# Weaving the last layers of two batches into one instruction order

## The chip, the cores and the metric

The kernel runs on one core of a Trainium2 chip. The metric is the device time of one execution in microseconds (us): 4720.15 us is the median of three runs (4719.32 to 4720.28). Engines: PE is TensorE (matmuls and transposes; PEld its weight loads), ACT is ScalarE, DVE is VectorE, POOL is GpSimd, SP issues the DMAs.

## The reference, cut to what matters

Four batches of 750 frames (748 tokens after the first layer, T = 748, width 128) pass through four layers of attention and feed-forward. The change touches what follows layer 1, per batch:

```python
# layer 2 attention ("additive"): every query/key pair gets a small tanh network
hid  = tanh(hq[:, :, None, :] + hk[:, None, :, :] + b1)        # 16 hidden values a pair
attn = softmax(Q @ K.T / sqrt(128) + einsum(hid, W2) + b2)     # 748 x 748
h   += attn @ V
# layer 2 experts: 8 experts (128 -> 512 -> 128, gelu, gelu), gated for the whole batch
# layer 3 attention ("last"): 8 heads of width 128, causal, softmax
h   += concat_heads(softmax(q @ k.T) @ v) @ Wo.T
# layer 3 experts ("last experts"): 8 experts (128 -> 256 -> 128, relu), gated per token
```

Before each block the running sum `h` is normalised and transposed. Everything here is fp32.

## The kernel before, in words

Tokens lie in NT = 6 tiles of 128 (the last has 108), and a [128, 748] product is made in two halves of 384 and 364 columns. Every engine has one instruction queue, run in order; semaphores join them, and the order of each queue is written out by hand.

The front layers and the layer-1 experts fill the first 3020 us; the change leaves them alone. Then comes a hardware loop `tail` of B = 4 turns, one batch a turn, with four parts strictly one after the other:

- **part 0**: normalise `hn`, products `hq2`, `hk2`, `q2`, `v2`; `additive_attention`: per query tile, ACT makes 16 tanh planes [128, 748] (each holds 8 queries x 16 hidden values, `tanh_order`, L1436), and PE sums each plane into the 32 rows of the scores it belongs to (L942, a 128x32 weight; the target rows are `32 * (g // 4)`). Planes are taken in the order g = 0, 4, 8, 12, 1, 5, ...; each is consumed by two matmuls (the two halves of the scores) before the next one. Then softmax, transposes (L953) and product with V (L961). Then pooling and gating for the experts.
- **part 1**: layer-2 experts. `stream` runs PE jobs (L839) over four PSUM banks, ACT applies gelu (L1379); the weights come by DMA into two buffers. A loop of four turns with two experts each.
- **part 2**: `third_attention`: per head, the query product (L823, `fused` weights), values (L868), six score tiles (L881, diagonal mask L890), DVE maximum (L1728), ACT exponential (L1399), transposes of the probabilities (L901), DVE and ACT copy them (L1736, L1407), product with V (L911), DVE adds to `h` (L1745). Scores are made two tiles ahead of their use, in two pairs of banks; transposes have two banks of their own.
- **part 3**: last experts, relu (L1379 again), turned back by PE (L857) and added by DVE (L2151).

`fuse` (L987 to L992, ACT L1450) multiplies the query and key weights of each head, and the value and output weights, into `fused`: four heads (EARLY) behind part 0, four (LATE) behind part 1, in every turn of the loop. POOL computes the reciprocal root of each normalisation (L711), four a batch.

Of the kernel before, what the change touches and what calls it, by code (L numbers as in the profile page):

```python
# [29 lines left out]
P = 128  # L30
NT = (T + P - 1) // P
TP = NT * P
H0 = 3 * P
# [42 lines left out]
def offsets(parts):  # L76
# [12 lines left out]
    "operand_ready0", "operand_ready1", "xn_turned", "xn_copied", "first_merged", "h_final", "h_stored", "h_ready", "front_done", "h_spilled", "front_spilled",  # L89
    "xt_loaded", "base_loaded", "merged", "merged_spilled", "h_loaded", "hn_loaded", "hn_free", "out_free", "wts_free", "wts_loaded0", "wts_loaded1",  # L90
# [15 lines left out]
    "logits_ready", "exps_ready",  # L106
]

# [86 lines left out]
def causal_keys(tile):  # L195
# [5 lines left out]
LAYER3 = Attention(NT, lambda u: causal_keys(u % NT), float(D) ** -0.5, product_mask="diagonal",  # L201
                   summed=True)
# [143 lines left out]

def fuse_steps(heads):
# [10 lines left out]
def additive_groups(u):  # L358


    groups = min(P, T - u * P + 7) // 8
    order = [4 * (i % 4) + i // 4 for i in range(P // 8)]
    return [(g, g % 4 == 3 or g == groups - 1) for g in order if g < groups]


ADDITIVE = [additive_groups(u) for u in range(NT)]
AHEAD = 5
BETWEEN = 7


def tanh_order():

    for u in range(NT):
        for i, (g, _) in enumerate(ADDITIVE[u]):
            yield "tanh", u, g
            if u and i == AHEAD - 1:
                yield "exp", u - 1, None
    yield "exp", NT - 1, None
# [7 lines left out]
def audio_tower(nc, A, per_turn):  # L386

    with ExitStack() as ctx:
# [79 lines left out]
        hn = tokens(q_room[:, TPAD:TPAD + TP])  # L468
# [37 lines left out]
        fused = shared[:, E * W3_END:E * (W3_END + 2 * P)].rearrange("p (e n) -> p e n", e=E)  # L506
        natural = shared[:, E * (W3_END + 2 * P):E * (W3_END + 2 * P) + 6 * P].rearrange("p (k n) -> p k n", k=2)
# [36 lines left out]

        def keys_in(j):
            return min(P, T - j * P)

        def tanh_ring(i):

            return (hid[:, 0, :], hid[:, 1, :], masked[:, 0, :], masked[:, 1, :], flat(x1), flat(att), flat(y),  # L550
                    merged[:, 0:TP])[i % 8]
# [10 lines left out]
        def _(sp):  # L562
# [7 lines left out]
            def load(src, at, k):  # L570

                sp.wait_ge(S["wts_free"], n.take("wts_free"))
                sp.dma_start(wts[:, k, 0:src.shape[2]], src[at, :, :]).then_inc(S[f"wts_loaded{k}"], 16)
# [38 lines left out]
            def load_hn(b):  # L612
                sp.dma_start(flat(hn), saved["h"][b, :, :]).then_inc(S["hn_loaded"], 16)
# [10 lines left out]
            def experts():  # L624
                for e in range(-1, RUN + 1):
# [4 lines left out]
                    for what, *at in expert_steps(e):  # L630
# [22 lines left out]
                        elif what == "merge" and at[1] == 0 and e < RUN:  # L653
# [7 lines left out]
                            if e == RUN - 1:  # L661

                                sp.wait_ge(S["ring_done"], n.now("ring_done"))
                                load_hn(0)
                n.take("wr_free")
# [11 lines left out]
            def tail(b, following=None):  # L677
                sp.wait_ge(S["shared_free"], n.take("shared_free"))
                sp.dma_start(third_w, A["l3"].rearrange("e p n -> p e n")).then_inc(S["third_loaded"], 16)
                for stage, src in (("l2", A["l2"]), ("l4", A["l4"])):  # L680
                    with n.loop(sp, stage, E // 2, S["loop_entered"]) as pair:
                        for k in range(2):
                            load(src, pair * 2 + k, k)
                    if stage == "l2" and following is not None:
                        sp.wait_ge(S["hn_free"], n.take("hn_free"))
                        load_hn(following)
                sp.wait_ge(S["h_final"], n.take("h_final"))
                full = (NT - 1) * P
                sp.dma_start(A["out"][b, 0:full, :].rearrange("(t p) d -> p t d", p=P), h[:, 0:NT - 1, :])\
                    .then_inc(S["h_stored"], 16)  # L690
                sp.dma_start(A["out"][b, full:T, :], h[0:T - full, NT - 1, :]).then_inc(S["h_stored"], 16)
                sp.wait_ge(S["h_stored"], n.take("h_stored", 32))
                sp.sem_inc(S["out_free"], 1)

            spill_merged(STAGES[-1])
            sp.sem_inc(S["out_free"], 1)
            with n.loop(sp, "tail", B - 1, S["loop_entered"]) as b:
                tail(b, b + 1)
            tail(B - 1)
# [3 lines left out]
        def _(pool):  # L703
# [81 lines left out]
            with n.loop(pool, "tail", B, S["loop_entered"]):  # L785
                power(4)
# [3 lines left out]
        def _(pe):  # L790
            n = Tally("tensor", per_turn)

            def turn(src, waited=False):

                if not waited:
                    pe.wait_ge(S["operand_ready"], n.take("operand_ready"))
# [33 lines left out]
            def stream(jobs, start, first=0):  # L830

                base = n.now("feat_done") - first
                for i, (reads, terms, (lo, hi)) in enumerate(jobs, first):

                    pe.wait_ge(S["feat_done"], base + (max(reads, i - 3) if reads else i - 3))
                    for c, (w, rhs) in enumerate(terms):
                        mm = pe.matmul(ps[:, (start + i) % 4, 0:hi - lo], w, rhs[:, lo:hi],  # L839
                                       start=(c == 0), stop=(c == len(terms) - 1))  # L840
# [1430 lines left out]
```

## Time and profile before

| | us |
|---|---|
| median of three runs | 4720.15 |
| the profiled execution | 4720.54 |
| its span on the core | 4718.2 |
| PE busy in it | 4292.0 (91%) |
| ACT busy | 2950.9 (63%) |
| DVE busy | 2785.4 (59%) |

The profile has a page with shares, a strip of 40 slices, and views of the trace: groups by line, a timeline, waits, and busy times of a stretch. Matmul ends are modelled and neighbouring records overlap, so PE's rate is read from start to start. An fp32 matmul stands as two records, an fp32 transpose as one.

### The profile page before, as it was taken

Reading aid. Unit: us, or ns where it says so; the run is one execution under the profiler, and the core shown is the slowest. Engines: PE = TensorE matmul, PEld = TensorE weight load, DVE = VectorE, ACT = ScalarE, POOL = GpSimd, SP = SyncE. Lnnn points to the kernel's source line nnn. Section 1 sums busy time; section 2 is a strip of 40 time slices with the busy share of each in tenths; the row PEclk is TensorE's granted clock in tenths of the full one; section 3 lists DMA queues with packets and bytes.
Section 4 is the critical chain, followed back from the end, with each engine's and each line's share of the span. In section 5 each row is a group of like instructions: output and inputs, shape, how many; then the busy total and the mean of one; then the engine's idle time right before and its main releaser. Section 6 shows DMA issues by size and latency. Waiting matters only on the chain.

```text
span 4718.2 us, 71767 instructions
## 1 busy us (share of the span) xinstructions
PE 4292.0 (91%) x24891; PEld 2384.9 (51%) x24891; DVE 2785.4 (59%) x6486; ACT 2950.9 (63%) x6401; POOL 692.9 (15%) x466
## 2 busy tenths in 40 slices
PE   6888689999999999999999999789888888988988
PEld 4555434444444444444444444356645654664566
DVE  5655477777777777777777777223422542252244
ACT  2222257777777778777777777574475447537644
POOL 0000212222222222222222322100000000000000
PEclk9868789999999999999999999899999989999999
DMA  2000142424334243342424322100011010001000
GB/s 105 1 27 1 34 48 41 52 38 55 54 46 59 38 55 50 50 58 39 55 45 55 54 38 34 42 14 22 10 36 35 1 45 5 31 1 45 27 5 17
DMA packets 101136, 173.34 MB, mean 37 GB/s; under 512 B 18816, under 2 KB 75568, under 8 KB 100400
## 3 DMA queue, kind: packets, MB, share of 16 engines
q1 hardware_dynamic: 100784, 168.82, 20.7%
q8 instruction: 199, 3.26, 0.3%
q14 instruction: 153, 1.25, 0.1%
HBM read 86.66 MB, written 7.82 MB: 20 GB/s over the span
## 4 chain that ended last, share of the span: by engine, by line
PE 54%; issue 35%; DVE 6%; ACT 1%; DVEq 1%; POOL 1%; DMA 1%; POOLq 0%; SPq 0%; ACTq 0%
PE ps L1032 12%; PE ps L1068 12%; PE ps L1042 10%; PE ps L1102 4%; PE ps L1111 3%; PE ps L1023 2%; PE ps L868 2%; PE ps L1131 2%; DVE peaks L1851 1%; PE ps L823 1%; PE ps L881 1%; PE ps L1092 1%; PE ps L839 1%; PE ps L1136 1%; PE ps L911 1%
## 5 line engine op out<-in xcount | busy, mean ns | idle before, releaser
L1851 DVE TENSOR_REDUCE peaks<-ps 128x1 f32<-128x748 f32 (+1 forms) x1536 | 1408.2, 933 | 482.7 <-PE ps L1042 460.4
L1469 ACT ACTIVATE masked<-ps 128x384 f32<-128x384 f32 (+3 forms) x1536 | 683.4, 486 | 196.2 <-PE ps L1032 184.1
L1469 ACT ACTIVATE probs<-ps 128x384 f32<-128x384 f32 (+1 forms) x1536 | 662.5, 484 | 73.9 <-PE ps L1032 73.5
L711 POOL TENSOR_TENSOR rstd<-var,minus_half 128x6 f32<-128x6 f32 x104 | 138.3, 1330 | 2998.6 <-DVE var L1670 2998.6
L1032 PE MATMUL ps<-shared 98*128 98x384 bf16 (+3 forms) x1536 | 447.3, 327 | 4.4 <-ACT probs L1469 1.7
L1032 PE MATMUL ps<-q_stack,k_stack 98*128 98x384 bf16 (+3 forms) x1536 | 450.0, 328 | 1.0
L1042 PE MATMUL ps<-k_stack,q_stack 96*128 96x374 bf16 (+1 forms) x1536 | 380.6, 329 | 36.0 <-DMA k_stack<-parts 21.6
L1042 PE MATMUL ps<-shared 96*128 96x374 bf16 (+1 forms) x1536 | 372.1, 323 | 9.0 <-DVE peaks L1851 8.3
L1032 PEld LDWEIGHTS ps<-shared 98*128 98x128 bf16 (+1 forms) x1536 | 147.9, 103 | 336.6 <-ACT masked L1469 125.8
L1032 PEld LDWEIGHTS ps<-q_stack,k_stack 98*128 98x128 bf16 (+1 forms) x1536 | 149.6, 103 | 328.7 <-ACT masked L1469 121.2
L839 PE MATMUL ps<-xnT,wts 128*128 128x384 f32 (+1 forms) x768 | 270.8, 503 | 5.0 <-DVE lg L2110 3.3
L1399 ACT ACTIVATE probs<-ps,neg_top 128x128 f32<-128x128 f32 (+3 forms) x216 | 131.8, 613 | 221.1 <-DVE neg_top L1730 221.1
L839 PE MATMUL ps<-hid,wts 128*128 128x384 f32 (+1 forms) x768 | 251.7, 478 | 0.0
L1379 ACT ACTIVATE hid<-ps,wts 128x364 f32<-128x364 f32 (+1 forms) x384 | 211.1, 575 | 44.1 <-PE ps L839 31.8
L1042 PEld LDWEIGHTS ps<-k_stack,q_stack 96*128 96x128 bf16 (+1 forms) x1536 | 154.7, 105 | 158.2 <-DVE peaks L1851 43.1
L1042 PEld LDWEIGHTS ps<-shared 96*128 96x128 bf16 (+1 forms) x1536 | 155.8, 104 | 117.9 <-issue 38.5
L1102 PE MATMUL ps<-attT,wr 128*128 128x364 f32 (+1 forms) x512 | 208.2, 491 | 2.7
L839 PEld LDWEIGHTS ps<-xnT,wts 128*128 128x128 f32 x768 | 150.1, 200 | 105.1 <-issue 19.4
L839 PEld LDWEIGHTS ps<-hid,wts 128*128 128x128 f32 x768 | 145.9, 190 | 95.4 <-ACT hid L1379 0.7
L881 PE MATMUL ps<-xnT,QT 128*128 128x320 f32 (+5 forms) x512 | 174.2, 449 | 2.3 <-ACT QT L1367 2.3
L911 PE MATMUL ps<-V,probsT 128*128 128x128 f32 x936 | 151.1, 304 | 26.0 <-DVE probsT L1736 25.9
L1728 DVE TENSOR_REDUCE top<-ps 128x1 f32<-128x128 f32 (+3 forms) x216 | 129.0, 597 | 75.3 <-PE ps L890 67.5
(389 smaller groups left out, 7609.5 us busy)
## 6 DMA issues: line engine op xcount, KB each, us to landing
shared<-parts SPq DMA_DIRECT2D x192, 187.0 KB, 9.2
wr<-in_l SPq DMA_DIRECT2D x32, 580.5 KB, 3.5
q_stack<-parts SPq DMA_DIRECT2D x96, 187.0 KB, 7.9
k_stack<-parts SPq DMA_DIRECT2D x96, 187.0 KB, 10.2
wts<-in_l SPq DMA_DIRECT2D x32, 514.5 KB, 3.3
wrow<-in_l_rows SPq DMA_DIRECT2D x32, 320.0 KB, 4.1
wts<-in_l SPq DMA_DIRECT2D x32, 257.5 KB, 2.6
shared<-in_l SPq DMA_DIRECT2D x4, 2048.0 KB, 9.8
```

What stands on the lines that cost most here:

```text
L711: pool.tensor_tensor(lane.rstd, lane.var, minus_half[:, :], ALU.pow).then_inc(S["rstd_ready"], 1)
L839: mm = pe.matmul(ps[:, (start + i) % 4, 0:hi - lo], w, rhs[:, lo:hi], start=(c == 0), stop=(c == len(terms) - 1))
L881: mm = pe.matmul(ps[:, 2 * (u % 2) + a, 0:width], query(u), key(u)[:, a * width:(a + 1) * width], start=True, stop=masked_by is None, skip ...
L911: mm = pe.matmul(ps[:, 6 + u % 2, 0:dv], probsT[:, j, :], value(u, j), start=(j == 0), stop=(j == len(tiles) - 1))
L1032: pe.matmul(out[0:m, 0:hi - lo], k_stack[k][0:STACK + SHIFT, head, j * P:j * P + m], q_stack[k][0:STACK + SHIFT, head, lo:hi], start=True, ...
L1042: mm = pe.matmul(out[0:m, a, 0:T // 2], q_stack[k][0:STACK, head, j * P:j * P + m], k_stack[k][0:STACK, head, a * T // 2:(a + 1) * T // 2] ...
L1068: mm = pe.matmul(ps[at:at + PLACE, 6, 0:hi - lo], V32[x % 2][0:m, j, head, :], probs_ring(SIDE * b + i)[0:m, 0:hi - lo], start=(j == 0), s ...
L1102: pe.matmul(out[:, 0:hi - lo], wr[:, WR_UP + f * P:WR_UP + (f + 1) * P], attT[:, lo:hi], start=True, stop=True).then_inc(S["ring_ready"], 1)
L1111: mm = pe.matmul(out[:, 0:hi - lo], wr[:, WR_DOWN + f * P:WR_DOWN + (f + 1) * P], hid[:, f, lo:hi], start=(f == 0), stop=(f == FT - 1))
L1379: act.activation(dst[:, lo:hi], ps[:, (start + i) % 4, 0:hi - lo], final if f is None else func, bias=bias[-1] if f is None else bias[f]). ...
L1469: act.activation(probs_ring(u)[0:m, 0:hi - lo], src[0:m, 0:hi - lo], ACT.Exp, scale=float(HD) ** -0.5).then_inc(S["ring_done"], 1)
L1851: v.tensor_reduce(peaks[0:m, g, j, head:head + 1], src[0:m, :, 0:T // 2], XY, ALU.max)\
```

## The change

The loop is replaced by one list, `TAIL`, from which every engine writes its queue. Each part is a list of steps with costs; `woven` merges two lists so that both advance at the same relative pace. The order is: part 0 and part 1 of batch 0 alone; then for b = 1, 2, 3 part 2 of batch b-1 with part 0 of batch b, and part 3 of b-1 with part 1 of b; at the end part 2 and part 3 of batch 3 alone. No hardware loop is left.

```diff
+def woven(*parts):
+    out = []
+    for b, part in parts:
+        steps, done = tail_steps(b, part), 0.0
+        whole = sum(cost for _, cost in steps)
+        for step, cost in steps:
+            out.append(((done + cost / 2) / whole, b, part, step))
+            done += cost
+    return [(b, part, step) for _, b, part, step in sorted(out, key=lambda entry: entry[0])]
+
+def tail_order():
+    order = woven((0, 0)) + woven((0, 1))
+    for b in range(1, B):
+        order += woven((b - 1, 2), (b, 0)) + woven((b - 1, 3), (b, 1))
+    return order + woven((B - 1, 2)) + woven((B - 1, 3))
```

Two sets of buffers and semaphores (`tails`, `TailLane`) serve even and odd batches. What else changes:

- **fuse** is a step of batch 0 alone; `fused` then stays in SBUF, and the last experts' weights (`fourth_w`) are loaded once instead of per batch.
- **additive attention**: 24 `add` steps, four tanh planes each (a "quad"), in three slots of four buffers. ACT's step: four tanh; in the second of each tile two tanh, the exponential of the tile before, two tanh. PE now takes a whole quad for the first half of the scores, then for the second. PSUM: one pair of banks for scores (5, 6), one bank (7) for transposes and results:

```diff
+                    pe.wait_ge(S["hidden_ready"], n.take("hidden_ready"))
+                    for a in range(2):
+                        for i, (g, last) in enumerate(quad):
+                            at = 32 * (g // 4)
+                            mm = pe.matmul(ps[at:at + 32, 5 + a, 0:T // 2],
+                                           add_w[:, 32 - 8 * (g % 4):64 - 8 * (g % 4)],
+                                           tanh_buffers[4 * slot + i][:, a * T // 2:(a + 1) * T // 2], start=False,
+                                           stop=last, skip_group_check=True)
+                    mm.then_inc(S["hidden_used"], 1)
```

- **last attention**: 67 steps `last(i)` over a list of entries, for each head score 5, 3, 4, 0, next query, 1, next value, 2, alternating between slot X (banks 0 and 1) and slot Y (bank 2). In step i PE does: product with V of entry i-3, first-half transposes of entry i-2, entry i itself, second-half transposes of entry i-2. Transposes share one bank (4), results one bank (3). ACT in step i: copy of the second-half transposes of i-2, then the exponential (or copy) of entry i. DVE: add of i-3, copy of i-2, maximum of i. The values of a head are copied by one ACT instruction instead of six:

```diff
+                    what, e, u = last_entry(i - 3)
+                    if what == "score":
+                        slot_done(LAST_AT["value", e, None])
+                        taken(k)
+                        if tiles > 3:
+                            pe.wait_ge(S[f"taken1_{k}"], n.take(f"taken1_{k}"))
+                    spread(0)
+                    if what is not None and slot_before(i) is not None:
+                        slot_done(slot_before(i))
+                    spread(1)
```

- **layer-2 experts** keep four banks (4 to 7); **last experts** get three (0 to 2) and one (3) for turning back. Their relu and gelu now alternate in ACT's queue.
- SP's queue: the next batch's `hn` is loaded when its lane's buffer is free (`hn_free_k`), then eight expert weights, then the store of the batch before.

## Rows read from the trace of the kernel before

**Rows 1.** The page, busy time of each engine over the span.
```profile
PE 4292.0 (91%) x24891; PEld 2384.9 (51%) x24891; DVE 2785.4 (59%) x6486; ACT 2950.9 (63%) x6401; POOL 692.9 (15%) x466
```
**Rows 2.** Timeline of POOL in the tail: start us, length, engine, line, operation.
```profile
3026.66 1.33 POOL L711 TENSOR_TENSOR rstd<-var,minus_half 128x6 f32<-128x6 f32 x1 [4.42 <-DVE var L1670]
...
3450.33 1.32 POOL L711 TENSOR_TENSOR rstd<-var,minus_half 128x6 f32<-128x6 f32 x1 [67.18 <-DVE var L1670]
...
3873.33 1.32 POOL L711 TENSOR_TENSOR rstd<-var,minus_half 128x6 f32<-128x6 f32 x1 [66.74 <-DVE var L1670]
```
**Rows 3.** Stretches, parts 0 to 3: us; PE, PEld, DVE, ACT, POOL busy; PEclk; DMA.
```profile
3444.50:3567.80 123.30, 101.02 (x578) 52.65 (x578) 32.35 (x102) 91.15 (x128) 2.64 (x2) 0.91 0.09 30
3567.80:3661.50 93.70, 90.60 (x290) 55.58 (x290) 17.89 (x61) 54.10 (x95) 1.32 (x1) 0.94 0.14 44
3661.50:3801.50 140.00, 124.17 (x807) 97.54 (x808) 76.89 (x240) 59.75 (x186) 0.00 (x0) 1.00 0.00 1
3801.50:3868.00 66.50, 56.65 (x216) 38.16 (x214) 23.91 (x102) 29.26 (x51) 1.32 (x1) 0.90 0.09 24
```
**Rows 4.** Busy time by stretch, columns as above: tanh stretch; layer-2 experts at full clock.
```profile
3464.50:3544.50 80.00, 78.67 (x472) 37.05 (x472) 12.59 (x32) 77.96 (x102) 0.00 (x0) 1.00 0.00 1
...
3571.70:3651.20 79.50, 79.44 (x251) 47.05 (x249) 9.72 (x25) 45.98 (x81) 0.00 (x0) 1.00 0.15 48
```
**Rows 5.** PE's timeline where two parts join (idle before it in brackets).
```profile
3453.45 1.54 PE L799 MATMUL ps<-const,xn 128*128 128x128 f32 x6 [10.31 <-DVEq L1656]
...
3566.42 0.60 PE L1280 MATMUL ps<-const,spread 128*128 128x8 f32 x2 [5.83 <-DVEq L1656]
...
3808.39 1.54 PE L799 MATMUL ps<-const,xn 128*128 128x128 f32 x6 [5.86 <-DVEq L1656]
```
**Rows 6.** PE's timeline, first and last record of a `fuse` (half clock).
```profile
3655.00 1.54 PE L987 MATMUL ps<-const,shared 128*128 128x128 f32 x6 [0.65 <-DVE h L1714]
...
3660.75 0.39 PE L992 MATMUL ps<-shared 128*128 128x128 f32 x2
```
**Rows 7.** ACT's timeline, tanh planes back to back.
```profile
3480.67 0.90 ACT L1436 ACTIVATE y<-hid,hqb 128x748 f32<-128x748 f32 x1
3481.48 0.90 ACT L1436 ACTIVATE merged<-hid,hqb 128x748 f32<-128x748 f32 x1
```
**Rows 8.** Busy time of line L942 alone over the tanh stretch.
```profile
3463.00:3545.00 82.00, 62.75 (x376) 25.25 (x376) 1.00 0.00 1
```
**Rows 9.** PE's timeline in the experts of layer 1: four column groups together (L1068).
```profile
2591.03 0.82 PE L1068 MATMUL ps<-probs,V 128*32 128x364 f32 x8
2591.78 0.69 PE L1032 MATMUL ps<-q_stack,k_stack 98*108 98x364 bf16 x3
```
**Rows 10.** PE's timeline over one head of the last attention.
```profile
3668.40 0.33 PE L901 MATMUL ps<-const,probs 128*128 128x128 f32 x1 [0.71 <-ACT probs L1399]
...
3675.57 0.21 PE L890 MATMUL ps<-maskb,identb 128*128 128x108 bf16 x1
...
3678.37 1.38 PE L911 MATMUL ps<-V,probsT 128*128 128x128 f32 x10 [1.08 <-DVE probsT L1736]
...
3685.93 0.33 PE L901 MATMUL ps<-const,probs 128*128 128x128 f32 x1 [0.71 <-ACT probs L1399]
```
**Rows 11.** DVE's timeline in that head.
```profile
3675.82 0.94 DVE L1728 TENSOR_REDUCE top<-ps 128x1 f32<-128x748 f32 x1 [0.46 <-PE ps L890]
```
**Rows 12.** ACT's timeline in that head.
```profile
3677.02 0.88 ACT L1399 ACTIVATE probs<-ps,neg_top 128x748 f32<-128x748 f32 x1 [1.53 <-DVE neg_top L1730]
```
**Rows 13.** ACT's timeline, table loads in front of a gelu and none before a relu.
```profile
3568.77 1.28 ACT L1379 ACT_TABLE_LOAD   x1
...
3817.66 0.24 ACT L1444 ACTIVATE ex<-lg 128x48 f32<-128x48 f32 x1 [7.22 <-DVE lg L1818]
3818.96 0.58 ACT L1379 ACTIVATE hid<-ps,wts 128x384 f32<-128x384 f32 x1 [1.06 <-PE ps L839]
```
**Rows 14.** DVE's timeline at the turn of the loop `tail`.
```profile
3448.17 1.25 DVE L1662 BATCH_NORM_STATS2 stats<-q_stack 128x6 f32<-128x128 f32 x6 [3.68 <-issue]
```

More of the change, by code:

```diff
@@ L355, with additive_quads @@
 EARLY, LATE = tuple(range(E // 2)), tuple(range(E // 2, E))
-def additive_groups(u):
+def additive_quads(u):
     groups = min(P, T - u * P + 7) // 8
[L362 to L378, printed above, removed]
+    return [[(g, g % 4 == 3 or g == groups - 1) for g in range(q, groups, 4)] for q in range(4)]
@@ new lines, with last_attention_entries @@
+ADDITIVE = [additive_quads(u) for u in range(NT)]
+TANH_SLOTS = 3
+X_SLOT, Y_SLOT = 0, 1
+def last_attention_entries():
+    out = [("query", 0, None), ("value", 0, None)]
+    for e in range(E):
+        for u in (5, 3, 4, 0):
+            out.append(("score", e, u))
+        if e + 1 < E:
+            out.append(("query", e + 1, None))
+        out.append(("score", e, 1))
+        if e + 1 < E:
+            out.append(("value", e + 1, None))
+        out.append(("score", e, 2))
+    return out
@@ L381, in cut @@
+TAIL = tail_order()
+@dataclass
+class TailLane:
+    k: int
+    h: object
+    hn: object
+    xn: object
+    xT: object
+    QT: object
+    V: object
+    probs: object
+    probsT: object
+    stats: object
+    mv: object
+    var: object
+    rstd: object
+    half_sum: object
+    pooled: object
+    spread: object
+    hqb: object
+    top: object
+    neg_top: object
+    total: object
+    rtotal: object
+    gating: object
+    gates: object
+    gcol: object
 def cut(ap, n):
@@ L675, in _ @@
             experts()
[L677 to L687, printed above, removed]
+            spill_merged(STAGES[-1])
@@ L692, in tail @@
                 sp.wait_ge(S["h_stored"], n.take("h_stored", 32))
[L693 to L699, printed above, removed]
+                sp.sem_inc(S[f"out_free_{k}"], 1)
+            sp.wait_ge(S["shared_free"], n.take("shared_free"))
+            sp.dma_start(third_w, A["l3"].rearrange("e p n -> p e n")).then_inc(S["third_loaded"], 16)
@@ L784, in _ @@
             experts()
-            with n.loop(pool, "tail", B, S["loop_entered"]):
-                power(4)
+            for b, part, (what, *at) in TAIL:
+                if what == "normalise":
+                    power(1, tails[b % 2])
         @block.tensor
@@ L1537, in experts @@
                 n.take("stacks_loaded", 2 * len(Q_PARTS) * 16)
-            def columns(k, at, count):
-                return [wts[:, k, at + i:at + i + 1] for i in range(count)]
             act.wait_ge(S["consts_loaded"], 48)
@@ L1704, in tok_measured, with attention @@
                             v.bn_stats(lane.stats[:, tile, :], dst[:, tile, :])
[L1706 to L1717 removed]
+            def attention(spec, dst):
                 def peak(u):
```

1043 lines of the change are left out of this document (698 added, 345 removed).

## The prediction

> **What bounds the kernel now.** I read the page first: PE is busy 91% of the span, ACT and DVE about 60% [rows 1]. An average over unlike stages says little, so next came the tail's period. POOL does four roots per batch; the first of each batch stands at 3026.66, 3450.33 and 3873.33, so one turn takes 423.5 us and the four turns 1694 of the 4718 us [rows 2]. Then I cut one turn into its four parts [rows 3]: 123.3 us (part 0), 93.7 (part 1), 140.0 (part 2), 66.5 (part 3). They are bound differently. In the tanh stretch ACT is busy 77.96 of 80.00 us [rows 4], one plane each 0.81 us [rows 7]; in the layer-2 experts PE is busy 79.44 of 79.50 [rows 4]; in part 2 PE is busy 124.2 of 140.0 and ACT 59.8. Between the parts PE stands idle for the normalise-and-turn chain and the gating: 10.31, 5.83 and 5.86 us [rows 5], and the granted clock of these stretches is 0.90 to 0.94 instead of 1.00 [rows 3]: after each such gap PE runs a while at 1.2 GHz. So the tail has two kinds of slack: an ACT-bound part 0, and the joints.
>
> **The change, part by part.** What the weave can reach is PE's own work, so I sum PE's time for each woven pair.
>
> Tanh sums. Before, the 376 records of L942 keep PE busy 62.75 us beside ACT [rows 8]. In the new order the four matmuls of a quad go to four different groups of 32 columns, as the four matmuls (eight records) of L1068 do: the next instruction starts 0.75 us after the first [rows 9], for 364 columns in fp32. A step is two such quads; the second needs no change back to the full array, so 1.45 us a step, and 24 steps are 35 us. The bounds are 24 x 1.3 = 31 (no cost for entering and leaving) and 62.75 (no gain from the order); I take 35 because L1068 has the same shape of weight and the same order. The Trainium skill, TensorEngine Tiling (Array Packing), Key Properties, says that changing the tiling mode drains TensorE, which speaks against sprinkling quads between full-array matmuls. The 0.75 us holds such a change already, so the trace prices it below 0.15 us.
>
> The rest of part 0: PE is busy 101.0 us there [rows 3]; less 62.75 for L942 and about 4 for `fuse` (an estimate from its 6 us at half clock [rows 6]) that leaves 34. The clock of 0.91 over 123.3 us means 22 us at half clock [rows 3], mostly idle; I take some 6 us of work in them, which takes half at full clock, so 31.
>
> Woven pair W1 (part 2 of b-1 with part 0 of b): 124 + 35 + 31 = 190 us of PE. ACT: 59.8 + 91.2 - about 5 (`fuse` and a table load) - 5 (values copied at once) = 141 us; DVE: 76.9 + 32.4 = 109 us. PE bounds it, at 74% load of ACT.
>
> In-order queues cost something on top. A score tile of 748 columns goes PE to DVE in 0.25 us (3675.57 to 3675.82 [rows 10, 11]), DVE to ACT in 1.20 (3675.82 to 3677.02 [rows 11, 12]), and ACT needs 0.88: about 2.4 us until its transposes can start, behind it on ACT now four tanh, 3.24 us. I walked one query tile of part 0 (add steps 2, 3, 0, 1 and 2 again) against one head (8 steps of `last`, 15.4 us of PE work: 17.53 from start to start less the waits of 1.08 and 0.71 [rows 10], rounded down for shorter ones). PE's work is 28 us and its waits come to 3.3: 2.3 us where the transposes of a short tile wait for an exponential queued behind the add step in which ACT also does its own exponential and PE has nothing (q = 1), and twice 0.7 where the product with V follows the second-half transposes with nothing between. That is 12%, of 190 us some 22; with part of such waits already in the 124, I take 20. W1 = 210 us. Bounds: 190 (no wait) and 190 + 24 x 2 = 238 (every add step keeps PE waiting for what is left of 3.24 us after PE's own 1.45, rounded up).
>
> Woven pair W2 (part 3 of b-1 with part 1 of b): layer-2 experts 79.5 + 2 = 81.5 us [rows 4]; part 3 has 56.65 us busy, and its clock of 0.90 means 13 us at half clock [rows 3], of which about 12 are work and count half, so 51; turning back and one normalisation 1.7. Together 134 us of PE against 54.1 + 29.3 = 83 of ACT. Waits: at its end the normalisation of batch b (5.86 us of idle PE in the open today [rows 5]) has only some 4 us of the other lane's work beside it, and then the next pair waits for the copy: 4 us; 3 more for a gating exponential among the gelus and PSUM rings of four and three banks. W2 = 141, bounds 134 and 155 (all joints of today's parts 1 and 3 stay open, some 20 us).
>
> Alone at the start: part 0 and part 1 of batch 0. ACT still bounds the tanh stretch; PE now has pauses in it, which is worth 0 to +8 us if the clock falls there. I take 217 + 2 = 219. Alone at the end: part 2 of batch 3 has one bank for transposes, so the product with V waits for ACT's copy in three tiles of a head and twice for DVE's; a walk over one head (waits of 0.8, 0.7, 0.7, 0.7 and 0.4 us where 2.1 stand now) gives 18.5 us for 17.53, +8 us, bounds 0 and +16. Part 3 keeps its 66.5 (three banks are enough: a matmul takes PE 79.44 / 128 = 0.62 us [rows 4], an activation 0.58 [rows 13], and PE is two jobs ahead). So 140 + 8 + 66.5 = 214.5.
>
> `fuse` once instead of four times removes about 6 us from first to last record at half clock [rows 6], of which most lies under the normalisation chain; in the pairs it is simply left out of the sums. The loop's turn, 3.68 us of DVE idle for nothing [rows 14], goes too and is part of the joints. The loads of `third_w` and of the last experts' weights per batch go; the layer-2 weights have the same two buffers and DVE frees them as before. SP's new waits (`hn_free_k`, then eight loads, then the store) queue nothing that is needed sooner than a whole pair later: cost nothing, and 5 us a pair if a load were late.
>
> **The sum**, against the profiled execution: 219 + 3 x (210 + 141) + 214.5 = 1486.5 for 1694, 207.5 less. The profiled execution took 4720.5 (span 4718.2, 2.3 around it), the median is 4720.15, so I predict 4720.5 - 207.5 = 4513 us.
>
> **The rivals.**
> *No waits in the weave.* The quad and the other lane cover each other's round trips: W1 = 190, W2 = 134. For it: ACT is at 74%. Against: tanh blocks of 3.24 us stand ahead of exponentials that PE needs within about two steps. 3 x 27 = 81 us below the forecast: 4432.
> *ACT's queue paces the weave.* Every add step delays the other lane: W1 = 238 and W2 = 155. That is 3 x 42 = 126 above: 4639. For it: PE gets nothing in the q = 1 step, and there the walk loses most.
> *No gain from weaving.* If each pair ran like its parts in sequence, only the loop turns and three fuses would go: 4 x 3 + 3 x 3 = about 20 us, 4700. For it speaks only that both lanes share all three queues.
> *Table reloads, slower.* In W2 relu and gelu alternate on ACT. A load takes 1.28 us [rows 13] and stands wherever the function asked for is not in the loaded set. The last experts have 16 relu and 16 identity steps a pair, each between gelus: up to 64 loads, 82 us of ACT, and with the jobs waiting in turn nearly as much of PE. It decides from 207.5 / (3 x 1.28) = 54 loads a pair; at 64 the time is 4513 + 246 = 4759. Against it: relu follows an exponential without a load [rows 13]. No row has relu right after gelu. The Trainium skill, ScalarE: Activation LUTs, Table sets, says that relu, copy and identity are in every set, and also to batch calls by set; by its 1283 ns plus about 1380 ns of drain a reload would be twice as dear, 4513 + 510 = 5023 by 64 of them. The first of its sentences speaks for the change, and the trace agrees as far as it goes.
>
> **How the numbers follow.** Forecast (4460 to 4590, the pairs each within some 20 us of their sums) 0.70; no waits 0.11; ACT paces 0.13; no gain 0.03, half of it within 0.2%; slower 0.03. The range 4440 to 4620 holds the forecast, most of the first rival and half of the second, about 0.84 less what I overlook. A measurement of this kernel can tell 0.2%, 9 us, from no change. Faster 0.95, same 0.02, slower 0.03.
>
> **What would show it.** In the changed kernel's stretches: the first pair W1 of about 210 us with PE busy nearly throughout, granted clock 1.00 and ACT about two thirds busy; the records of the tanh sums starting four together, 1.4 to 1.5 us a step; no table load between relus and gelus; no idle of PE over 3 us except at the ends of W2. Waits of PE on ACT's `probs` over 2 us behind the q = 1 steps prove the walk right. The prediction is wrong if quads don't run together (W1 up by 27 us), if PE waits in most steps, or if half clock persists within the pairs.

## The result, and the profile after

The changed kernel takes 4617.27 us (median of four runs, 4615.43 to 4618.23) where the kernel before takes 4719.73 on the same chip: a ratio of 0.9782, 95% interval 0.9766 to 0.9799. That is 102.5 us less. The forecast was 207 us less, 4513; its range (4440 to 4620) just holds the result.

The page shows the same shares as [rows 1], of a shorter span:

```profile
PE 4177.5 (91%) x24723; PEld 2308.0 (50%) x24723; DVE 2783.5 (60%) x6451; ACT 2903.9 (63%) x6181; POOL 693.1 (15%) x466
```

So it tells nothing of where the gain is. POOL's roots cut the tail again, as in [rows 2] (timeline of POOL, columns as there):

```profile
3025.11 1.33 POOL L892 TENSOR_TENSOR rstd<-var,minus_half 128x6 f32<-128x6 f32 x1 [4.27 <-DVE var L2413]
3135.58 1.32 POOL L892 TENSOR_TENSOR rstd<-var,minus_half 128x6 f32<-128x6 f32 x1 [109.14 <-DVE var L2413]
...
3625.62 1.32 POOL L892 TENSOR_TENSOR rstd<-var,minus_half 128x6 f32<-128x6 f32 x1 [7.71 <-DVE var L2413]
...
4008.09 1.32 POOL L892 TENSOR_TENSOR rstd<-var,minus_half 128x6 f32<-128x6 f32 x1 [7.71 <-DVE var L2413]
...
4381.43 1.32 POOL L892 TENSOR_TENSOR rstd<-var,minus_half 128x6 f32<-128x6 f32 x1 [133.04 <-DVE var L2413]
4550.89 1.32 POOL L892 TENSOR_TENSOR rstd<-var,minus_half 128x6 f32<-128x6 f32 x1 [168.14 <-DVE var L2413]
```

Two pairs together take 4008.09 - 3625.62 = 382.5 us; the forecast had 210 + 141 = 351, and before a batch took 423.5. Part 0 alone takes 110.5 us between the first two roots, part 2 alone 169.5 between the last two; the kernel before had 103.2 and, between the like roots, 148.1. The stretches (columns as in [rows 3]) are part 0 of batch 0 alone; pair W1 (part 2 with part 0) from its first to its last step, the second of the three; pair W2 (part 3 with part 1); part 2 of batch 3 alone:

```profile
3025.11:3135.58 110.47, 79.32 (x557) 40.76 (x558) 24.55 (x68) 87.17 (x117) 1.33 (x2) 0.83 0.08 29
...
3623.70:3861.60 237.90, 200.07 (x1358) 135.67 (x1359) 112.36 (x359) 141.62 (x264) 2.65 (x2) 0.94 0.03 9
...
3862.00:3999.90 137.90, 135.28 (x465) 83.98 (x464) 33.30 (x121) 77.65 (x134) 2.15 (x2) 0.97 0.08 24
4381.43:4550.89 169.46, 135.79 (x817) 101.20 (x817) 83.54 (x267) 55.97 (x145) 1.32 (x2) 0.95 0.01 3
```

The forecast booked the joint behind W2 with W2, so the two sums compare like this: W2 with its joint takes 138 + 6 = 144 for 141, and W1 takes 238 from its first step to its last for 210, three times. The miss is in W1; the stretch alone at the end adds 20 (235 for 214.5). TensorE's six longest waits in W1 (engine, tile and line; what it waited for; us in total, times, longest):

```profile
PE ps L1543 <- ACT parts L1953: 8.3, 11, 1.8
PE ps L1557 <- DVE parts L2555: 6.7, 9, 3.3
PE ps L1543 <- DVE parts L2555: 5.8, 4, 4.1
PE ps L1557 <- ACT parts L1964: 4.7, 3, 2.7
PE ps L1579 <- ACT y L1973: 2.7, 1, 2.7
PE ps L1428 <- ACT probs L1898: 2.4, 1, 2.4
```

L1543 is the product with V, L1557 the transposes, L1579 the scores of part 2; ACT L1953 and DVE L2555 copy the transposed halves, ACT L1964 is the exponential. No single wait carries it, and busy time hides a good part, since the ends of matmuls are modelled. So I read the distances between the starts of PE's instructions and took off each the time of its size at full clock (0.83 us for 1000 columns of an fp32 record: records of 384 columns start 0.32 us apart, 0.64 at half clock; a quad of sums counts a quarter of that, as its four column groups run together). W1 in us (own calculation from the trace):

```
work by size, full clock   168
extra at half clock          9
small gaps (under 0.15)     11
waits over 0.15             49    (61 of them; before, 20 in the 140 us of part 2)
```

Without its waits the pair is 168 + 9 + 11 = 188 us, and the floor of the forecast was 190. The waits were put at 20. By place, the first 27 us of the second pair (from the end of the experts before) hold 12.6 us of work, and its last 34 us 16.7 us of work and 14 of waits. VectorE's timeline shows the last wait (14 lines of the gating and one of part 2 left out):

```profile
3854.70 0.41 DVE L2555 COPY parts<-ps 128x256 f32<-128x256 f32 x1
3855.03 0.16 DVE L2149 SCALAR_TENSOR_TENSOR lg<-pick,lg 128x8 f32<-128x8 f32 x1
...
3858.59 0.18 DVE L2142 TENSOR_TENSOR gates<-ex,m 128x8 f32<-128x8 f32 x1
...
3859.41 0.35 DVE L2549 SCALAR_TENSOR_TENSOR k_stack<-ps,wrow,k_stack 128x128 f32<-128x128 f32 x1 [0.41 <-issue]
3859.68 0.55 DVE L2555 COPY parts<-ps 128x384 f32<-128x384 f32 x1
```

and TensorE's the price:

```profile
3855.78 0.49 PE L1557 MATMUL ps<-const,parts 128*128 128x128 f32 x3
3860.38 1.62 PE L1543 MATMUL ps<-y,parts 128*128 128x128 f32 x6 [4.11 <-DVE parts L2555]
```

Transposes started at 3855.78 are copied only at 3859.68, because batch b's gating, small operations every 0.24 us, stands ahead in the queue.

### The profile page after: what moved, and what is told of

It reads as the page before. It is cut to its first block, busy times and chain, and to the rows that moved or that the text cites. A ratio compares the mean times of both kernels' runs of the same rounds, so it can differ in the third digit from the quotient of the medians.

```text
span 4615.9 us, 66988 instructions
## 1 busy us (share of the span) xinstructions
PE 4177.5 (91%) x24723; PEld 2308.0 (50%) x24723; DVE 2783.5 (60%) x6451; ACT 2903.9 (63%) x6181; POOL 693.1 (15%) x466
## 4 chain that ended last, share of the span: by engine, by line
PE 76%; DVE 9%; ACT 6%; issue 6%; DVEq 2%; POOL 1%; DMA 1%; POOLq 0%; PEld 0%; PEldq 0%; SPq 0%; ACTq 0%
PE ps L1131 12%; PE ps L1167 12%; PE ps L1487 11%; PE ps L1141 10%; PE ps L1201 4%; PE ps L1210 3%; PE ps L1122 2%; PE ps L1543 2%; PE ps L1018 2%; PE ps L1419 2%; PE ps L1579 2%; DVE peaks L2180 2%; PE ps L1230 2%; PE ps L1003 1%; PE ps L1031 1%
## 5 line engine op out<-in xcount | busy, mean ns | idle before, releaser
L1878 ACT ACTIVATE hid<-ps,wts 128x384 f32<-128x384 f32 (+1 forms) x256 | 146.3, 573 | 63.7 <-PE ps L1487 52.4
L1210 PE MATMUL ps<-hid,wr 128*128 128x364 f32 (+1 forms) x512 | 171.1, 477 | 0.0
L1487 PE MATMUL ps<-hid,wts 128*128 128x364 f32 (+1 forms) x512 | 169.5, 478 | 0.0
L1791 ACT ACTIVATE hid<-ps,wr 128x384 f32<-128x384 f32 (+1 forms) x256 | 139.9, 572 | 44.0 <-PE ps L1201 40.7
L1167 PE MATMUL ps<-masked,shared 128*32 128x384 f32 (+3 forms) x1536 | 160.5, 490 | 0.6 <-ACT masked L1750 0.6
L1167 PE MATMUL ps<-probs,V 128*32 128x384 f32 (+1 forms) x1536 | 160.5, 490 | 0.0
L1167 PE MATMUL ps<-masked,V 128*32 128x384 f32 (+3 forms) x1536 | 160.5, 490 | 0.0
L1167 PE MATMUL ps<-probs,shared 128*32 128x384 f32 (+1 forms) x1536 | 160.5, 490 | 0.0
L1487 PEld LDWEIGHTS ps<-hid,wts 128*128 128x128 f32 x512 | 96.8, 190 | 62.1
```

The source lines that it names most:

```text
L1167: mm = pe.matmul(ps[at:at + PLACE, 6, 0:hi - lo], V32[x % 2][0:m, j, head, :], probs_ring(SIDE * b + i)[0:m, 0:hi - lo], start=(j == 0), s ...
L1210: mm = pe.matmul(out[:, 0:hi - lo], wr[:, WR_DOWN + f * P:WR_DOWN + (f + 1) * P], hid[:, f, lo:hi], start=(f == 0), stop=(f == FT - 1))
L1487: mm = pe.matmul(ps[:, bank, 0:hi - lo], w, rhs[:, lo:hi], start=(c == 0), stop=(c == len(terms) - 1))
L1791: act.activation(dst[:, lo:hi], src[:, 0:hi - lo], ACT.Gelu, bias=wr[:, bias:bias + 1])\
L1878: act.activation(dst, src, func, **more).then_inc(S[f"feat_done_{k}"], 1)
```

## The experiments

Each starts from the changed kernel or from a better version named there. "Pair" is W1 from its first to its last step, the second of three. The kernel before took 4717.7 to 4720.0 in these comparisons.

**What is the weave worth by itself?** e1_sequence:

```diff
-        order += woven((b - 1, 2), (b, 0)) + woven((b - 1, 3), (b, 1))
+        order += woven((b - 1, 2)) + woven((b - 1, 3)) + woven((b, 0)) + woven((b, 1))
```

> The new parts, quads and single fuse are kept, but nothing is woven: part 0, 1, 2, 3 of each batch in turn. If the missing gain went into the new steps of parts 0 and 2 (alone in the changed kernel: start 219.3 us between POOL's roots, part 2 169.5 where 148.1 stood before), a batch costs 219.3 + 169.5 + 66 = 455 us, some 8 less where fuse is left out, and the total is 4617 + 4 x 455 - 24 - (219 + 3 x 382.5 + 235) = 4812 us: slower than before by about 90. If the new steps cost nothing and the weave itself brought only 100, it lands at about 4700 (before, less three fuses and the loop's turns).

4808.55 us, ratio 1.0189 (1.0169 to 1.0210). So the change is two changes: new parts that cost 90 us, and a weave that gives 191. The parts that were made fit for the weave cost nearly half of what it gives. Part 2 in its new order, alone, takes 166.2 us between roots (3239.22 to 3405.43) for 148.2 before.

**ScalarE's queue.** e2_half_tanh leaves out two of the four tanh planes of a step:

```diff
+                        if i % 2:
+                            continue
                         last = act.activation(tanh_buffers[4 * (s % TANH_SLOTS) + i][:, 0:T], ...
```

> ScalarE computes two of the four tanh planes of each step and leaves the others out (TensorE adds all four buffers as before, so its work is the same). A block of tanh ahead of an exponential is 1.6 us instead of 3.2. Theory 1 (TensorE's waits in the pair of part 2 and part 0 come from ScalarE's in-order queue): the pair falls from 244 us to 215-222, its waits from 48 to about 20. Theory 2 (the waits come from part 2's own order: product with V right behind the second-half transposes of the same tile): the pair falls by at most 8, to 236 or more. Part 0 alone at the start falls by some 30 us in both.

4583.28 us; the pair 231.2, 7 us less. ACT's busy time in it fell by 36:

```profile
3598.50:3829.70 231.20, 200.57 (x1358) 137.45 (x1359) 112.38 (x359) 105.21 (x218) 2.64 (x2) 0.94 0.03 9
```

By its length this speaks against theory 1; the waits alone say otherwise, see below.

**Part 2's own order.** e3_late_weigh: in a step PE did product with V of i-3, first transposes of i-2, filling of i, second transposes of i-2. Now the filling comes first, `copied` waits for both copies of i-3 (the bank is free then), and `weigh_last`, the product with V of i-3, stands between the two halves:

```diff
+        def last_probsT(lane, i):
+            return (lane.probsT, lane.xn)[LAST_UNIT[i] % 2]
...
                     if what is not None:
                         mm.then_inc(S[f"slot_ready_{k}"], 1)
                         n.take(f"slot_done_{k}")
+                    copied()
+                    spread(0)
+                    weigh_last()
                     spread(1)
```

with VectorE's copy and maximum ahead of its addition, and a second buffer for the transposed probabilities. Order and buffer are tested together.

> In each step of the last attention the product with V of tile i-3 moves from the head of the step to a place between the two transposes of tile i-2, and the filling of tile i to the head (so that a copy always has a matmul job over it); the transposed probabilities get a second buffer (the normalised rows, idle there). Theory 2 (part 2's own order): part 2 alone falls from 169.5 us to about 150, each woven pair from 244 to 225-230, total 4617 - 19 - 3 x 16 = 4550. Theory 1 (ScalarE's queue): part 2 alone falls just so, the pairs stay within 5 us each, total 4590 to 4598. If the wait is on the exponential's round trip instead, nothing changes or it gets slower by some us.

4587.29 us, ratio 0.9720 (0.9704 to 0.9736). Part 2 alone fell from 169.5 to 151.9 us between roots (4369.33 to 4521.26): that cause is shown. The pairs moved by little, the three of them by -3, -1 and -7 us: about what theory 1 says, which e2 had just spoken against. But the waits of PE in them did fall, by 8 us a pair. What took that back is the clock: the granted clock of the second pair is 0.91 for 0.94, and the extra at half clock rose from 9 to 16 us.

**The joint.** e4_joint: part 1 spread over 86% of W2, and the next batch's first normalisation inside it.

> Only the order of steps at the end of the pair of part 3 and part 1 changes: part 1 of the later batch ends after 86% of the pair, so that its normalisation lies beside the other batch's last experts, and the first normalisation of the batch after it is made there too. Theory 3 (the joint costs 5 us of idle TensorE and then 17 us at half clock): each of three joints loses 8 to 12 us, total 4617 - 25 to -35 = 4582 to 4592, and the clock at the start of the pair stays at full. Rival: the last experts alone in the rest of the pair wait for each other as the joint did, and the total stays within 5 us.

4615.95 us, nothing. The 5 us of idle PE before the joint became one wait of 2.0, one of 1.3 and one of 2.7, and PE's half clock still lay over the opening of W1, where query, value and first scores wait for each other's copies.

**The order of the planes.** e5_planes:

```diff
-                    for a in range(2):
-                        for i, (g, last) in enumerate(quad):
+                    for i, (g, last) in enumerate(quad):
+                        for a in range(2):
```

> TensorE adds the planes of a quad one after the other, two matmuls each (as before the change), and not the four planes for one half and then for the other: the same 376 instructions in another order. The forecast's term: the sums take 62 us of TensorE where they take 35 now, so each woven pair becomes 27 us longer (244 to 271, total 4617 + 3 x 27 = 4698), while part 0 alone at the start is bound by ScalarE and, with TensorE busy nearly throughout and its clock at full, gets 3 to 7 us shorter. Rival: the quads don't run together and nothing changes.

4622.19 us, 5 us more and not 81; the intervals of the two ratios overlap (0.9778 to 0.9817 and 0.9766 to 0.9799), so the 5 us are not shown either. A quad still takes what it took:

```profile
4038.05 1.49 PE L1419 MATMUL ps<-hid,add_w 128*32 128x374 f32 x16 [0.60 <-ACT hid L1914]
```

**The closing.** e6_closing, order alone:

```diff
+    move(("gate", 1), (b, 1, ("up2", 0, 1)))        # last gating piece into W2
+    order.insert(mark + 1, (b, 0, ("pooled",)))      # pooling on VectorE one step of part 2 later
```

> Theory 4: at the end of a pair of parts 2 and 0, VectorE's queue holds part 0's pooling (waits for ScalarE, then 2.6 us) and gating (16 small operations, 4 us) ahead of the copies that part 2 needs. Only the order changes: the last piece of the gating goes into the next pair, where VectorE has room; the pooling's vector work goes behind one more step of part 2. Expected: TensorE's waits of 3.3 and 4.1 us there fall to under 1, 5 to 7 us a pair, total 4617 - 18 = 4596 to 4602. If the clock or the round trips set the end instead, under 2 us a pair.

4603.52 us (4599.49 to 4608.22), 14 less. Somewhat under the forecast of 15 to 21; the longest waits of the transposes and of the product with V on VectorE's copy fell from 3.3 and 4.1 us to 0.9 and 1.0, so the cause is shown.

**The opening.** e7_opening, order and two banks:

```diff
+        move((b, 0, ("measure", "hn")), (old, 3, ("back4", 5, 1)))
+        move((b, 0, ("normalise", "hn")), (old, 3, ("down4", 6, 1)))
+        move((old, 3, ("back4", 7, 0)), (old, 3, ("down4", 7, 1)))
+        move((new, 1, ("normalise", "h")), (old, 3, ("back4", 7, 0)))
+        move((b, 0, ("turn", "hn")), (new, 1, ("normalise", "h")))
+    move((b, 0, ("mixed", 0)), (b - 1, 2, ("last", 0)))
+    move((b, 0, ("mixed", 1)), (b - 1, 2, ("last", 1)))
```

> Theory 5: at the start of such a pair TensorE has 12.6 us of work in 27 us, because query, value and score products of part 2 wait for each other's copies while nothing of part 0 is ready. Order only (and two other banks for one transposed tile): the later batch's first normalisation is made in the pair before, its turning and its first products stand between part 2's first three steps. Expected 5 to 8 us a pair from waits and half clock, total 4617 - 20 = 4595 to 4602. Rival, as in the run on the joint: the time moves elsewhere, under 2 us a pair.

4605.76 us (4602.57 to 4611.28), 11.5 less, 4 a pair: half of what I expected, more than the rival.

**All three.** e8_ends_late: e3, e6 and e7 together.

> Both orders above, and the later product with V with its second buffer. If the three causes add up: 4587 - 18 - 20 = 4549, the pair of parts 2 and 0 at about 226 us. If they share the same slack (the pair is then held by something else, such as the exponential's way over three engines): 4565 or more.

4548.96 us, ratio 0.9639 (0.9623 to 0.9655), 68 less, where the three singly give 30, 14 and 11.5, together 55.5. The pair takes 225.

**Why the sums are cheap.** e9_one_group (`at = 0` for `at = 32 * (g // 4)`):

> All tanh planes are added into the first 32 rows of the scores (one column group of TensorE) and none into the other 96; so the output is not the reference's, but instructions, sizes and order stay. If matmuls of 128x32 weights are cheap (0.156 us each now) because four of them run in four different groups at once, eight of one group take 8 x 0.62 = 5 us instead of 1.25, a woven pair gets 24 x 3.7 = 89 us longer and the total is about 4617 + 3 x 85 + 60 (start) = 4930. If the narrow weight alone makes them cheap, nothing changes: 4617. The run in another order of planes changed nothing, which either reading allows, since neighbours in that order were still in two groups.

4953.59 us (one run), the pair 326.9 for 238. Timelines of PE over one step, first e9, then the changed kernel:

```profile
3862.02 1.45 PE L1419 MATMUL ps<-masked,add_w 128*32 128x374 f32 x4
3863.30 0.79 PE L1419 MATMUL ps<-att,add_w 128*32 128x374 f32 x2
3863.93 0.79 PE L1419 MATMUL ps<-attT,add_w 128*32 128x374 f32 x2
3864.55 1.42 PE L1419 MATMUL ps<-masked,add_w 128*32 128x374 f32 x4
...
3867.07 0.48 PE L1419 MATMUL ps<-KT,add_w 128*32 128x374 f32 x1
```
```profile
3705.14 0.51 PE L1419 MATMUL ps<-masked,add_w 128*32 128x374 f32 x2
3705.15 0.50 PE L1419 MATMUL ps<-att,add_w 128*32 128x374 f32 x1
3705.16 0.50 PE L1419 MATMUL ps<-attT,add_w 128*32 128x374 f32 x1
...
3706.11 0.48 PE L1419 MATMUL ps<-masked,add_w 128*32 128x374 f32 x2
```

Sixteen records (eight matmuls) take 5.05 us in one column group, 0.31 each, and about 1.3 in four groups, where four start within 0.02 us. The four groups are needed; e5 shows that the order within the quad does not matter. But the kernel before had the four groups too, and the order of e5. Its timeline of PE:

```profile
3481.62 0.50 PE L942 MATMUL ps<-y,add_w 128*32 128x374 f32 x1
...
3481.96 0.79 PE L942 MATMUL ps<-y,add_w 128*32 128x374 f32 x2
3482.43 0.50 PE L942 MATMUL ps<-merged,add_w 128*32 128x374 f32 x1
3482.59 0.47 PE L942 MATMUL ps<-y,add_w 128*32 128x374 f32 x1
```

The four records of plane `y` start 0.32 us apart, one behind the other in their group, and the next plane, in another group, starts 0.81 us after `y`, when ScalarE has made it: two groups at most are at work. Counted from start to start, L942 holds PE for 61 us in the 82 us of [rows 8], and L1419 for 31 us of a pair, with as many records (own calculation). So what the change adds is that PE gets four planes at once. No run hands the new kernel its planes one by one; this is read from the timelines alone.

**ScalarE's queue, again.** e10_best_half_tanh: the edit of e2 on e8.

> The version with both ends reordered and the later product with V (4549), with ScalarE computing only two of the four tanh planes of each step (the others left out). Theory 1, second test: with the other causes gone, what is left of TensorE's waits in the pair is ScalarE's queue: the pair of 366 us between starts falls by 10 to 15 us, total 4549 - 30 (start) - 3 x 12 = 4483. If the queue is no cause either, under 4 us a pair: 4510 or more.

4490.55 us, the pair 210.8: 14 us less than in e8, where the same edit gave 7 on the changed kernel. Part 0 alone at the start gave 11 us and not 30: ScalarE is not alone in bounding it. e11_best_split and e13_best_split2 keep all the tanh and only place it, in twos:

```diff
-        steps += [(("add", u, q), 3.95) for u in range(NT) for q in range(4)]
+        steps += [(("add", u, q, part), 1.975) for u in range(NT) for q in range(4) for part in range(2)]
```

In e11 the sums stand with the first two planes of a step, in e13 with the second.

> The same version with all its work; ScalarE's four tanh planes of a step are placed as two and two in the order, so that part 2's exponentials and copies find 1.6 us of tanh ahead of them and not 3.2. By theory 1 half of what the run with half the tanh shows: 3 to 6 us a pair, total 4549 - 9 to -18. If its queue is no cause: 4549 within 4.

> The version of 4549 us with ScalarE's four tanh planes placed as two and two, TensorE's sums and VectorE's work now behind the second two and not behind the first (in the run before they stood half a step too early, right behind the planes they add, and the pair got 13 us longer). Theory 1: 3 to 6 us a pair less, 4535 to 4543. If blocks of 1.6 us delay as blocks of 3.2: 4549 within 4.

e11: 4589.61 us, 41 more than e8, for the sums stood right behind the planes they need (the pair 238.5); it says how dear half a step too little between planes and sums is. e13: 4509.02 us, ratio 0.9558 (0.9542 to 0.9574), the pair 209.8, over twice what I expected. e14_best_split4, a plane a step:

> The same with every tanh plane a step of its own (blocks of 0.8 us). Theory 1: half as much again as the run in twos, 4530 to 4540; if the two last stages (the lag of the sums behind the planes) matter more, no better than in twos.

4526.22 us (4513.4 to 4526.69), pair 217.7: no better than in twos. Its waits are 4 us a pair longer than those of e13; which of them, and why, was not looked into. e15_best_no_tanh (e8, one plane of 8 columns a step):

> The version of 4549 us with ScalarE computing 8 columns of one plane per step instead of four planes (the rest of the tanh left out); TensorE's work is the same. It measures what a pair takes with no tanh ahead of anything: my floor was 190 us for the pair. By the work counted from sizes (170 us), 12 us of pitch between instructions and 10 us lost at half clock it is 192 plus what round trips remain: 200 to 208 from first to last step where the version takes 225. If it is 220 or more, ScalarE's tanh has no part in it.

4484.53 us (one run), the pair 207.2. So of e8's 225, the tanh ahead of other work costs 18, and placing it in twos takes 15 of them back. The stretches of e8, e13 and e15 (columns as above, ACT fourth of the busy times):

```profile
3607.70:3832.60 224.90, 198.37 (x1351) 134.98 (x1352) 104.32 (x323) 139.93 (x263) 1.32 (x1) 0.95 0.03 9
```
```profile
3593.10:3802.90 209.80, 191.73 (x1352) 131.25 (x1353) 104.58 (x323) 139.21 (x263) 1.32 (x1) 0.98 0.03 10
```
```profile
3578.60:3785.80 207.20, 192.48 (x1352) 132.19 (x1353) 104.28 (x323) 70.25 (x193) 1.32 (x1) 0.97 0.03 10
```

and PE's longest waits of e8 that are not the same in e15 (a wait of 2.9 us on VectorE and one of 2.2 on the exponential `probs` stand in both):

```profile
PE ps L1635 <- ACT parts L2023: 7.0, 4, 2.6
PE ps L1614 <- issue: 4.4, 4, 2.3
PE ps L1635 <- ACT y L2032: 3.5, 1, 3.5
```

in e15 (L1614 are the transposes, L1635 the scores; the 3.5 us of the value copy `y` are gone):

```profile
PE ps L1635 <- ACT parts L2025: 2.2, 2, 1.3
PE ps L1614 <- issue: 1.0, 3, 0.3
```

Is it the shorter block, or the greater distance of the sums from their planes? e18_best_lag keeps e13's place of the sums with the four planes in one block:

```diff
-                        if i * SHARES // 4 != part:
+                        if part:
...
-                    if quad and part == (len(quad) - 1) * SHARES // 4:
+                    if quad and part == 0:
```

> The version of 4549 us with the four planes left in one block of 3.2 us, a quarter step earlier, and TensorE's sums and VectorE's work a quarter step later, exactly where the run in twos (4509) has them. If that gain of 14 us a pair is the shorter block in ScalarE's queue (theory 1), it is 4549 within 8; if it is the greater distance between planes and sums, about 4515.

4562.14 us, 13 more than e8 and more than the 8 allowed: the distance is not it, it even costs; the shorter block is the gain. e17_split2_alone puts e13's edit on the changed kernel:

> The changed kernel with nothing but the placing of tanh in twos and the sums behind the second two (ends and product with V as in the change). In the version with reordered ends this gave 14 us a pair. If the causes hide one another (half the tanh gave 7 us a pair here and 15 there), it gives 5 to 8 us a pair, 4595 to 4602; if it is a cause by itself, 14 us a pair: 4575.

4590.02 us, ratio 0.9726 (0.9710 to 0.9742), 7 to 10 us a pair from root to root, 5 us under the first reading's lower end: about half of the 13 to 18 that it gives on e8.

**Why the same edit gives twice as much later.** The split of the pair into work, waits and half clock, made for every run in the same way (own calculation from the traces, mean of the three pairs, us):

| | pair | waits over 0.15 | extra at half clock |
|---|---|---|---|
| changed kernel | 237 | 50 | 8 |
| e2, half the tanh | 230 | 41 | 10 |
| e17, tanh in twos | 229 | 41 | 9 |
| e3, later product with V | 234 | 42 | 13 |
| e6, closing | 235 | 46 | 9 |
| e7, opening | 235 | 49 | 7 |
| e8, e3 + e6 + e7 | 226 | 36 | 12 |
| e10, half the tanh on e8 | 210 | 26 | 4 |
| e13, tanh in twos on e8 | 211 | 26 | 5 |
| e15, e8 almost without tanh | 205 | 23 | 4 |

The waits do not hide one another: half the tanh takes 8 us of them on the changed kernel and 10 on e8, the twos 8 and 9, and the 14 that e8 takes are about the sum of its three parts (8, 4 and 1). What differs is the clock. On the changed kernel the extra at half clock stays within 2 us or grows (by 4 in e3) when waits go; on e8 it falls by 6 to 8 us a pair (granted clock of the second pair 0.95 in e8, 0.98 in e13). Why it falls there and not before no run shows.

**The start.** e12_filler adds matmuls to bank 0 that nobody reads, in part 0 of batch 0: three where PE waits for the exponential, one behind the product with V.

```diff
+                    elif q == 1:
+                        filler(3)
```

> The changed kernel with work added: in part 0 of batch 0 alone TensorE multiplies four times per query tile a 128x512 block nobody needs (24 matmuls, 20 us at full clock) in its pauses. Theory 6: part 0 alone got 7 us longer because TensorE, idle between bursts, falls to half clock for 44 of 110 us, and its half-speed bursts hold up ScalarE. Then the clock stays at full there and part 0 alone falls from 110.5 to 103-106 us: total 4617 - 4 to -7. If the clock is no cause the filler costs 0 to 10 us.

4610.39 us (4606.13 to 4611.72), 7 less for 24 matmuls more. Part 0 alone takes 105.6. The tanh stretch of the changed kernel, then of e12, then of the kernel before:

```profile
3045.00:3125.00 80.00, 58.92 (x458) 27.14 (x454) 14.91 (x36) 73.10 (x95) 0.00 (x0) 0.87 0.00 1
```
```profile
3045.00:3125.00 80.00, 71.76 (x517) 31.49 (x508) 15.55 (x38) 74.33 (x98) 0.00 (x0) 1.00 0.00 1
```
```profile
3047.00:3127.00 80.00, 77.03 (x471) 38.16 (x468) 15.93 (x41) 72.97 (x96) 0.00 (x0) 1.00 0.00 1
```

**The sum of all.** e16_all: e13 with the filler.

> Both ends reordered, later product with V, tanh in twos, and the filler matmuls in part 0 of batch 0 alone. If all add up: the run in twos less 7, 4530 to 4537.

4500.40 us, ratio 0.9538 (0.9522 to 0.9554): the fastest kernel here that leaves nothing out, 219 under the kernel before and 117 under the change.

## Why the prediction was right or wrong

The kernel became faster by the way that was forecast, but by half as much: the result is 104 us over the forecast. Three times 27 us of that are W1, 20 the stretch alone at the end, and a few us each lie in the start and in W2.

*Waits of W1 (20).* This step failed: they are 49 us. The runs assign 14 of them to the two ends and the product with V (e8) and 9 to 10 more to the block of tanh (e13, e10); 23 are left even in e15. The walk over one head found the right places, the value copy among them (2.7 us), but a head in the middle of the pair has no ends. Part 0 opens and closes with chains (normalisation, first products, pooling, gating) in which it gives PE nothing and in which VectorE's queue holds up part 2. I had the joints as idle time in [rows 5] and let the weave absorb them all. The forecast also took part 2's new order for nearly free (+8 us where it stands alone), and e1 shows it at 18 us more than the old one. And its own terms were added wrongly: 2.3 and twice 0.7 are 3.7 and not 3.3, some 25 us for 22; that would have made W1 213.

*Half clock.* The sum counted it once, as a loss that goes with the joints, and took W1 at full clock. It stayed: 9 us a pair, and it fills 37 of the 110 us of part 0 alone (not 44, as the expectation of e12 has it) where it filled 9 of 103 before.

*Floor of W1 (190).* 188 measured, but by luck: at full clock it is 168 + 11 = 179, and the 9 us of half clock that the sum left out fill it up.

*Term of the sums (35 us).* Right: at full clock the instruction behind a quad starts at best 1.40 us after the quad's first (15 of the 36 quads that stand alone; own calculation), 34 us for 24 steps. The saving against the 61 us before is real as well. Its reason was half wrong: the four column groups are needed (e9, +89 a pair), the new order within a quad does nothing (e5), and the kernel before had the groups without the gain, since its planes came one by one.

*W2 (141).* Right: 138, and 144 with its joint. *Table loads.* Right: three in a W2 pair, none between relu and gelu, and the dearer price of a reload does not show either: each load takes the queue 1.28 us. ACT's timeline, `q_stack` and `y` being relus of the last experts and `masked` and `hid` gelus:

```profile
3887.88 0.24 ACT L1933 ACTIVATE wrow<-wrow 128x48 f32<-128x48 f32 x1
3888.14 1.28 ACT L1878 ACT_TABLE_LOAD   x1
3889.44 1.02 ACT L1878 ACTIVATE hid<-ps,wts 128x364 f32<-128x364 f32 x2
3890.35 0.56 ACT L1878 ACTIVATE q_stack<-ps,shared 128x364 f32<-128x364 f32 x1
3890.80 0.57 ACT L1878 ACTIVATE y<-ps,shared 128x364 f32<-128x364 f32 x1
3891.24 0.60 ACT L1878 ACTIVATE masked<-ps,wts 128x384 f32<-128x384 f32 x1
```

*Alone at the start (+2).* Part 0 alone took 7.3 us more; the price of the clock was taken from the lower end of its bounds (0 to 8). *Alone at the end (+8).* +21, beyond the bound of 16: the walk over one head said 18.5 us and measured was 18.7, but it was set against a head of 17.53, where the mean one was 17.2; the rest lies mainly at the opening of the part, where PE ran at half clock for most of 18 us. e3 shows that the order of the step, with its buffer, was the cause of most: 17.6 of it went.

*The rivals.* "ACT's queue paces the weave" (4639) is 22 us from the result, nearer than the forecast, and its W1 (238) is what the pair shows, though its W2 (155) is not. Its mechanism is only a part of it: 8 us of the 49 of waits by e2, and with the clock up to 18 us of the pair once other causes are mended (e15). The time alone would have proved it right.

e13, with part of its waits mended, has two pairs in 349.6 us (from root to root, 3587.97 to 3937.61) for the 351 forecast, and takes 4509 in all for 4513. That is no proof of the sum: it has 26 us of waits where the forecast had 20, and less work and half clock than the forecast's 190.

What stays open: the 23 us of waits that e15 still has, and whether the exponential's way over three engines sets them; what decides how long PE stays at half clock within a pair; why e14 is slower than e13; and what remains of the joint.

## What to carry to other kernels

A weave of two instruction orders is worth what its floor says only if the order is made for it: no long block of one lane's work in a shared queue ahead of short work that the bounding engine waits for, and no chain of small operations either. Walk the ends of the pair as well as its middle. And when the removal of one cause brings little time, look at the waits and at the granted clock apart before you drop it: half the tanh took 8 us of waits from the pair and gave 7 us of time while the pair stayed at its clock, and took 10 and gave 16 (14 in the second pair) once the ends were mended and PE ran less at half clock. Three edits together gave 68 us that gave 55 singly.

## What was not expected of the hardware

Work added to an idle TensorE made the kernel faster: with 24 matmuls more the granted clock of the stretch went from 0.87 to 1.00 and part 0 alone from 110.5 to 105.6 us. The same sums in small steps, one plane every 0.81 us, had kept it at 1.00 before. Eight fp32 matmuls with 128x32 weights run in 1.3 us in four column groups and in 5.05 in one, however they are ordered within the step, if all their planes are there; it was not expected that neighbours in one group would do no harm. And within a pair the clock moved the time almost as much as the waits did: of the 15 us that the pair lost from e8 to e13, 9 are waits and 6 half clock.
